# Two graph layers in one kernel: a block buffer for each graph, and the key sums folded to 64 rows

## The reference, cut to what matters

```python
def L0(h, adj):                       # attention over each graph
    q, k, v = h @ Wq.T + bq, h @ Wk.T + bk, h @ Wv.T + bv
    w = adj * exp(q @ k^T)
    return (w / sum(w, over keys)) @ v
def L1(h, adj):                       # W is 512 x 1024
    agg = (adj @ h) / max(sum(adj, -1), 1e-6)
    return relu(concat(h, agg) @ W.T)
h = relu(layernorm(x));  x = x + L0(h, adj)
h = relu(layernorm(x));  x = x + L1(h, adj)
```

## Time and profile before

| | us |
|---|---|
| median of 3 runs | 1941.86 (1937.01 to 1943.64) |
| profiled execution, its own time | 1942.48 |
| its span | 1940.4 |
| TensorE busy | 1892.7 (98%) |
| VectorE busy | 1579.6 (81%) |
| GpSimd busy | 1103.0 (57%) |
| ScalarE busy | 862.4 (44%) |
| SyncE's queue, as a share of 16 DMA engines | 57.2% |

### The profile page before, as it was taken

How to read it: one execution, slowest core, us unless ns; L and a number is a source line. 1 busy time by engine, 2 the same in 40 slices (tenths; PEclk the granted TensorE clock), 3 DMA queues, 4 the chain that set the end, 5 groups by cost and what they waited for, 6 DMA issues and landing times.

```text
span 1940.4 us, 29261 instructions
## 1 busy us (share of the span) xinstructions
PE 1892.7 (98%) x8956; PEld 1576.8 (81%) x8956; DVE 1579.6 (81%) x2649; ACT 862.4 (44%) x1453; POOL 1103.0 (57%) x1066
## 2 busy tenths in 40 slices
PE   8899999999999999999999999999999999999997
PEld 5778888888888888888788888888888888887885
DVE  6887888888788888888878888887888878888776
ACT  4344444444444445443445443444444454434442
POOL 4665565565565565655655655655655656546552
PEclk9999999999999999999999999999999999999999
DMA  6456656566656566555566555566555665555632
GB/s 222 148 189 212 210 181 196 188 203 207 210 178 190 198 205 204 192 198 173 189 208 219 188 194 184 191 211 211 179 191 194 204 203 194 197 173 184 211 125 87
DMA packets 190881, 370.69 MB, mean 191 GB/s; under 512 B 17936, under 2 KB 115216, under 8 KB 182672
## 3 DMA queue, kind: packets, MB, share of 16 engines
q1 hardware_dynamic: 190864, 370.48, 57.2%
HBM read 266.60 MB, written 103.81 MB: 191 GB/s over the span
## 4 chain that ended last, share of the span: by engine, by line
PE 49%; DVE 19%; DMA 17%; issue 8%; SPq 4%; POOL 2%; ACT 1%; DVEq 1%; POOLq 0%; ACTq 0%
PE bank L518 16%; PE bank L520 16%; PE bank L519 16%; DMA turned_store<-blocks 8%; DMA n_l<-t_store 8%; DVE y L1223 3%; SPq L263 3%; DVE x L1235 3%; DVE stats L1091 2%; DVE x L1227 2%; DVE g_full L1213 2%; DVE deg L1112 1%; DVE mean_sum L1096 1%; DVE blocks L1073 1%; DVE sums L1252 1%
## 5 line engine op out<-in xcount | busy, mean ns | idle before, releaser
L403 POOL TENSOR_TENSOR hT_l<-turned,hT_h 128x512 fp32r<-128x512 f32 x122 | 181.9, 1517 | 264.0 <-ACT hT_h L824 263.9
L242 POOL TENSOR_TENSOR w_l<-w,w_h 128x512 fp32r<-128x512 f32 x62 | 80.3, 1295 | 307.5 <-ACT w_h L857 307.5
L1073 DVE STREAM_TRANSPOSE blocks<-h 128x512 f32<-128x512 f32 x252 | 163.3, 685 | 110.3 <-DMA turned_store<-blocks 110.3
L518 PE MATMUL bank<-hT_h,n_h 128*128 128x512 f32 x512 | 200.9, 392 | 3.9 <-DVE hT_l L1164 2.8
L519 PE MATMUL bank<-hT_l,n_h 128*128 128x512 f32 x512 | 200.2, 391 | 0.0
L520 PE MATMUL bank<-hT_h,n_l 128*128 128x512 f32 x512 | 200.2, 391 | 0.0
L518 PE MATMUL bank<-wv_h,hT_h 128*128 128x512 f32 x512 | 199.6, 390 | 0.0
L519 PE MATMUL bank<-wv_l,hT_h 128*128 128x512 f32 x512 | 199.5, 390 | 0.0
L520 PE MATMUL bank<-wv_h,hT_l 128*128 128x512 f32 x512 | 199.3, 389 | 0.0
L399 POOL TENSOR_TENSOR xb<-x_in,bv_b 128x512 f32<-128x512 f32 x128 | 165.9, 1301 | 43.5 <-DVE x L1235 39.3
L843 ACT ACTIVATE kz_h<-bank,kp_bias 128x512 fp32r<-128x512 f32 x128 | 83.6, 675 | 207.5 <-PE bank L520 207.5
(11 more groups left out here) (152 smaller groups left out, 5394.9 us busy)
## 6 DMA issues: line engine op xcount, KB each, us to landing
turned_store<-blocks SPq DMA_DIRECT2D x126, 512.0 KB, 4.5
turned<-turned_store SPq DMA_DIRECT2D x504, 128.0 KB, 2.9
x_in<-x SPq DMA_DIRECT2D x32, 1024.0 KB, 5.3
n_h<-t_store SPq DMA_DIRECT2D x31, 1024.0 KB, 6.3
n_l<-t_store SPq DMA_DIRECT2D x31, 1024.0 KB, 8.3
out<-x SPq DMA_DIRECT2D x124, 256.0 KB, 2.0
n_h<-n_store SPq DMA_DIRECT2D x60, 512.0 KB, 4.6
n_l<-n_store SPq DMA_DIRECT2D x60, 512.0 KB, 5.9
```

Of the source, the lines that this page charges most:

```text
L242: engine.tensor_tensor(w_l[:, g], w[:, g], w_h[:, g].bitcast(F32), ALU.subtract).then_inc(w_split, 1)
L403: pool.tensor_tensor(by_blocks(hT_l, t), turned_tile(t), by_blocks(hT_h, t).bitcast(F32), ALU.subtract).then_inc(hT_split, 1)
L518: pe.matmul(dst, lh, rh, start=first, stop=False, skip_group_check=more)
L1073: nc.vector.transpose(blocks[:, :, :, t % NT, :].rearrange("p j c b -> p c j b"), h[:, t, :].rearrange("p (c j b) -> p c j b", c=DT, b=Q)) ...
```

## The change

There are now two block buffers, one for each graph. With it the stores and turns are no longer tied to each other: `turn_g` runs earlier in the step, both stores of a pair go out one after the other, and the T weights are loaded in two halves with a semaphore each. `degrees` moves behind the last `low_kp`, and `combine_s1` and `combine_s3` ahead of `weigh(i, 1)`. `combine_s2` moves ahead of `turn_h`, and both `turn_h` stand ahead of `low_v(i, 3)` and `sum_z`.

The buffers `z_full`, `sum_h` and `sum_l` are gone. `z_sum` (where p0 waits) lies in `g_full`. The key sums are folded: GpSimd adds the two tiles of keys (`fold_w`), ScalarE moves rows 64 to 127 beside rows 0 to 63 (`move_rows`), GpSimd adds them (`fold_rows`), ScalarE makes the high part in rows 0 to 63 of S1's place and GpSimd the low part in rows 64 to 127 (once p2 has read S1), and one matmul behind `az` tile 1 sums all 128 rows. In the first step and in `last_step` the sums come from four matmuls on `w_h` and `w_l` instead of two. `sum_inverses` moves ahead of the first result of layer 1.

```diff
-KP_BANK, V_BANK, SCORE_BANK = (5, 6, 2, 7), (3, 7, 0, 1), (0, 1)
-AZ_BANK, AV_BANK, SUM_BANK = (1, 0, 4, 2), (3, 1, 0, 4), 7
+KP_BANK, V_BANK, SCORE_BANK = (5, 6, 2, 3), (7, 3, 0, 1), (0, 1)
+AZ_BANK, AV_BANK, SUM_BANK = (1, 0, 4, 2), (7, 1, 0, 4), 6
...
+        sum_parts = hT_h[:, 0, :].rearrange("p (g n) -> p g n", g=G)
+        HALF = P // 2
...
-        with nc.sbuf_tensor("z_full", [P, ROUNDS, dim], F32) as z_full:
-            z_sum = (z_full[:, 0], z_full[:, 1])
-        sum_h, sum_l = sb("sum_h", [P, G, nodes], F32R), sb("sum_l", [P, G, nodes], F32R)
...
-        blocks = sb("blocks", [P, Q // 8, DT, NT, Q])
+        blocks = [sb(f"blocks{g}", [P, Q // 8, DT, NT, Q]) for g in range(G)]
...
+        def fold_w(engine, i, g):
             engine.wait_ge(w_split, G * i + g + 1)
             engine.tensor_tensor(w[:, g, 0, :], w[:, g, 0, :], w[:, g, 1, :], ALU.add).then_inc(w_summed, 1)
...
+            def move_g(j, between=None):
+                store_blocks(1, 0, g_turned, T * j + NT, g_stored)
+                if between is not None:
+                    between()
+                store_blocks(1, 1, g_turned, T * (j + 1), g_stored)
...
+                def next_x():
+                    sp.wait_ge(xb_done, T * (i + 1))
+                    load_x(i + 1)
+
+                move_g(j, next_x)
                 if is_first(i):
                     sp.wait_ge(n_stored, 32)
                     sp.wait_ge(t_stored, 64)
-                load_t(i)
+                sp.wait_ge(kp_psum, DT * (i + 1))
+                load_t(0)
+                load_t(1)
                 store_blocks(0, 0, h_turned, T * i + NT, h_stored)
-                load_n(j, 2)
-                load_n(j, 3)
-
                 store_blocks(0, 1, h_turned, T * (i + 1), h_stored)
-                load_turned(0, 0, h_moved)
-                sp.wait_ge(h_stored[1], 16 * (i + 1))
-                load_turned(0, 1, h_moved)
+                for g in range(G):
+                    reload_n(j, g, 16 * (i + 1))
+                    parts_made(j, g)
+                    load_turned(0, g, h_moved)
...
                 split_w(pool, i, 0)
+                fold_w(pool, i, 0)
                 scale_and_shift(0, i + 1, 0)
                 low_part(j, A11)
                 low_part(j, A12)
                 scale_and_shift(0, i + 1, 1)
-                low_part(j, S1)
-                low_part(j, S3)
                 split_w(pool, i, 1)
-                for m in (S2, A22, S4):
+                fold_w(pool, i, 1)
+                for m in (S1, S3, S2, A22):
                     low_part(j, m)
+                fold_rows(i)
                 low_sum(i)
+                low_part(j, S4)
                 for t in range(T):
...
+                pe.wait_ge(w_split, G * (i + 1))
+                every = bank[dst][:, :].rearrange("p (g n) -> p g n", g=G)
+                all_ones = ones[:, 0:1].to_broadcast([P, P])
+                for n, part in enumerate((w_h, w_l)):
+                    for c in range(NT):
+                        mm = pe.matmul(every, all_ones, part[:, :, c, :], start=(n == 0 and c == 0),
+                                       stop=(n == 1 and c == NT - 1))
                 mm.then_inc(sum_psum, 1)
...
+            def sum_folded(i, dst):
+                pe.wait_ge(sum_split, i)
+                every = bank[dst][:, :].rearrange("p (g n) -> p g n", g=G)
+                all_ones = ones[:, 0:1].to_broadcast([P, P])
+                pe.matmul(every, all_ones, sum_parts, start=True, stop=True).then_inc(sum_psum, 1)
...
-                pe.wait_ge(t_loaded, 32 * i)
+                pe.wait_ge(t_loaded[0], 32 * (j + 1))
...
+                pe.wait_ge(t_loaded[1], 32 * (j + 1))
...
                 az(j, 1, AZ_BANK[1])
+                sum_folded(i, SUM_BANK)
...
                 pe.wait_ge(ha0_done, ROUNDS * j + 1)
-                sum_weights(i, SUM_BANK)
-                pe.wait_ge(ha0_done, ROUNDS * j + 2)
                 av(i, 0, AV_BANK[0])
+                pe.wait_ge(ha0_done, ROUNDS * (j + 1))
...
             def high_sum(i):
-                act.wait_ge(w_summed, G * (i + 1))
-                nc.scalar.activation(sum_h[:, :, :], w[:, :, 0, :], ACT.Copy).then_inc(sum_high, 1)
+                act.wait_ge(sum_folded, i)
+                act.wait_ge(p_psum, PER_PAIR * (i - 1) + products_done(2, 1))
+                nc.scalar.activation(sum_parts[0:HALF], w[0:HALF, :, 0, :], ACT.Copy).then_inc(sum_high, 1)
+
+            def move_rows(i):
+                act.wait_ge(w_summed, G * i)
+                nc.scalar.activation(w[0:HALF, :, 1, :], w[HALF:P, :, 0, :], ACT.Copy).then_inc(sum_moved, 1)
...
+                act.wait_ge(combined, 4 * j + 3)
+                high_part(j, S2)
+                move_rows(i)
                 high_v(i, 3)
-                act.wait_ge(sum_psum, i)
                 copy_p0(j, 0)
                 copy_p0(j, 1)
-                act.wait_ge(combined, 4 * j + 3)
-                high_part(j, S2)
                 high_part(j, A22)
                 high_z(j, 0)
                 high_z(j, 1)
+                high_sum(i)
                 act.wait_ge(combined, 4 * j + 4)
-                act.wait_ge(p_psum, PER_PAIR * j + products_done(0, 1))
+                act.wait_ge(z_split, T * j + NT)
                 high_part(j, S4)
                 copy_u2(j, 0)
                 copy_u2(j, 1)
-                act.wait_ge(z_split, T * j + NT)
-                high_sum(i)
-                act.wait_ge(sum_split, i + 1)
+                act.wait_ge(sum_split, i)
                 copy_u3(j, 0)
                 copy_u3(j, 1)
...
                 low_kp(i, 0)
-                degrees(j)
+                turn_g(j, 0)
                 low_kp(i, 1)
-                dve.wait_ge(h_stored[1], 16 * i)
-                dve.wait_ge(hT_split, T * i)
-                turn_g(j, 0)
+                turn_g(j, 1)
                 low_kp(i, 2)
                 low_kp(i, 3)
-                turn_g(j, 1)
+                degrees(j)
                 low_v(i, 0)
                 weigh(i, 0)
...
                 layer0_stats(i + 1, 0)
-                weigh(i, 1)
-                layer0_stats(i + 1, 1)
-                low_v(i, 1)
                 if not is_first(i):
                     dve.wait_ge(x2_done, T * j)
                 combine_s1(j)
                 combine_s3(j)
+                weigh(i, 1)
+                layer0_stats(i + 1, 1)
+                low_v(i, 1)
                 low_v(i, 2)
-                dve.wait_ge(g_stored[1], 16 * (j + 1))
+                combine_s2(j)
                 turn_h(i + 1, 0)
+                turn_h(i + 1, 1)
                 low_v(i, 3)
-                combine_s2(j)
                 sum_z(j, 0)
                 sum_z(j, 1)
                 low_z(j, 0)
                 low_z(j, 1)
                 combine_s4(j)
-                dve.wait_ge(part_split, 7 * j + A22)
-                turn_h(i + 1, 1)
                 key_bias_of(i + 1, 0)
...
                 low_z(j, 3)
+                sum_inverses(i, SUM_BANK, T * (i + 1) + 1)
                 dve.wait_ge(deg_done, 3 * (j + 1))
                 sum_ha0(j, 0)
                 layer1_result(j, 0, AZ_BANK[0], x1)
                 sum_ha0(j, 1)
                 layer1_result(j, 1, AZ_BANK[1], x1)
                 layer1_result(j, 2, AZ_BANK[2], x1)
-                sum_inverses(i, SUM_BANK, T * (i + 1) + 1)
                 layer1_result(j, 3, AZ_BANK[3], x1)
...
+                layer1_result(j, 3, LAST_AZ_BANK[3], x1)
                 combine_s2(i)
-                layer1_result(j, 3, LAST_AZ_BANK[3], x1)
-                combine_s4(i)
             def final_step(i):
                 j = i - 1
+                sum_z(j, 0)
+                sum_z(j, 1)
+                low_z(j, 0)
+                low_z(j, 1)
+                combine_s4(j)
                 degrees(j)
-                sum_z(j, 0)
-                low_z(j, 0)
-                sum_z(j, 1)
-                low_z(j, 1)
                 sum_ha1(j, 0)
```

More of the change, by code:

```diff
@@ L919, in first_step @@
                 high_mix(T2)
-                for t in range(NT, T):
+                high_v(0, 2)
+                high_v(0, 3)
+                act.wait_ge(mixed, 4)
+                high_mix(T4)
+                act.wait_ge(v_psum, T)
+                for t in range(T):
                     high_hT(1, t)
```

174 lines of the change are left out of this document (84 added, 90 removed).

## The result

The changed kernel takes 2062.16 us (median of 4 runs, 2059.98 to 2063.63) against 1940.74 us on the same chip: ratio 1.063, 95% interval 1.060 to 1.065, so 121 us slower. The direction was forecast, the size wasn't: 1978 was said, with 2009 as the upper end.

A forecast was written before the change was run, and what follows sets the result against it. TensorE bounds the kernel. 29 x (57.73 + 2.6 - 58.90) = +41.5, step 1 about +1, the ends -6: +36.5 on 1942.5 gives 1979, or 1978 against the median; range 1907 to 2009, the forecast's own 1949 to 2009.

The forecast's parts named there:

- The wait for the T weights: TensorE at p2: earlier loads remove it, worth up to 0.94 us a step together with small waits for `kz_l`.
- The floor of 57.73: TensorE's step without any wait: 57.96 us falls to 57.73 as two matmuls for the sums become one.
- The ends: Outside the loop steps: 5 us off in `final_step` (0 to 7), 1 off in the first step (3 either way).
- rival 3: TensorE's clock also falls to 1.2 GHz behind each step's wait, costing 1.5 us: 2024 us; chance 0.10 (above 2009).
- the hold: VectorE beside GpSimd on shared ports: `combine_s2` 1.18 us instead of 0.69, two `low_z` 2.55; without both, z 2.5 earlier.
- they end at 23.4: VectorE: `combine_s1` and `combine_s3`, 0.69 us each, start at 22.0 after `turned` lands and end 23.4 us into the step.
- But then the four turns of h stand ahead of `sum_z`, 2.5 us: VectorE between `combine_s2` and `sum_z`: four turns add 2.5 us on the way to z, ready at 40.7.
- `move_rows` runs while ScalarE would wait: ScalarE: `move_rows` fits where the engine would wait for VectorE's turns, so it costs nothing.
- at nothing: Cost given to `degrees`, `sum_inverses`, `fold_w`, `move_rows`, n's return and S2 at p3; p3 0.5 us if cover is gone.
- if the turns aren't on the way to z: One of two signs that the forecast is wrong: h's four turns on VectorE don't delay z.
- Everything behind it moves along: Rest of the step behind TensorE's 2.6 us wait is counted from TensorE and shifts with it.
- 1901 + 30 w: Total time in us, with w as TensorE's wait per step, forecast at 2.6; even with before at w = 1.37.

The follow-up runs named there:

- fast order: Early transfers, two buffers and folded sums kept; VectorE, GpSimd, ScalarE and SyncE work reordered against the changed kernel: 1907.56 us, 0.992 to 0.996 of before.
- the turns back: Changed kernel with one pair of h's turns ahead of `combine_s2`, one behind `combine_s4`: 2113.03 us; with `copy_p0` also ahead of S2's high part: 2116.69 us.
- the other order: Changed kernel with `combine_s1` and `combine_s3` moved back behind `weigh` and the statistics of graph 1: 2003.63 us, 1.042 to 1.045 of before.

## Why the prediction was right and wrong

**Right.** TensorE is the bound and the question was whether operands come in time. The wait for the T weights went. The floor of 57.73 is met by the fast order to within 0.3 us. The ends: behind the loop 1940.4 - 1843.43 = 97.0 us became 2057.9 - 1965.48 = 92.4, so 4.6 won where 5 were said; ahead of it 1.4 us came, where 1 less at the start and 1 more in step 1 were said. The clock didn't fall: rival 3 would have been nearest to the time, for the wrong reason. (Its mechanism is real: it came with waits of 3 us in the runs with the turns back.) `combine_s2` lasts 1.76 us right behind S1's low part; there the hold was foreseen.

**Wrong 1: "they end at 23.4".** This is the step that failed first. `combine_s1` and `combine_s3` were costed at 0.69 us each, though by the order of the change GpSimd is at A11 and A12 in that very time, and the same prediction counts with the hold at two other places. They ended at 26.05: 0.9 from the transfer (22.9 for 22.0), 1.8 from the hold. Of these 2.65 us the weighing and statistics gave 0.9 back, since their last instruction, 1.00 us long in the step before the change, is no longer held (0.17). The rest went on: S1 at 33.05 (said: 31.4), `combine_s2` at 34.84 (33.3), z at 41.85 (40.7). At z 1.15 us are left of it, and the wait around `az` is 3.85 us instead of 2.6: about 37 us in 30 steps. Taking the hold away won 44 us, the other order 58.

**Wrong 2: the turns.** "But then the four turns of h stand ahead of `sum_z`, 2.5 us". They do, and they cost nothing (0 and 2.5 us in all, in two kernels). The prediction followed one chain, VectorE from `combine_s2` over the turns and `sum_z`. Another ended at the same time: ScalarE's S2, `move_rows`, v's high part, `copy_p0` and A22, then A22's low part and `fold_rows` on GpSimd, 0.55 us behind whose end z is ready. From the end of `combine_s2` it takes 34.84 to 41.85, 7.0 us, where the sum had 7.4 by its own way; that these are near is luck. The order on ScalarE alone costs 54 us. It had been put aside: "`move_rows` runs while ScalarE would wait", and p3 among the things costed "at nothing". By the prediction's own sign, it is wrong "if the turns aren't on the way to z".

**Wrong 3: "Everything behind it moves along".** `sum_inverses` was costed at nothing because TensorE has `az` tiles to do. But VectorE has no idle time from there to the next step, and who waits isn't the first `av` but the fourth, for the third y. 1.3 us a step, 38 us; 43 came back when the instructions went into idle time.

With w = 5.15 the prediction's own formula, 1901 + 30 w, gives 2056 of the 2062 measured. The sum was sound. Of the 84 us between 1978 and 2062, about 37 are the longer wait around `az` and 39 the wait at the fourth `av`, which had no term. The other 8 weren't traced.

## What to carry to other kernels

When an instruction moves, look at what runs beside it in its new place on every engine, not only at what stands ahead of it; a hold that is known at one place has to be asked for at each. Follow every chain that ends at the same wait, since removing work from one of two equal chains wins nothing (the turns), and a loss made of such chains shows its parts only when each is put back alone into a kernel without any. And an engine with an unbroken run of work has no harmless place within it: only idle time is free.
